# A rebuilt prologue: scale factors of the first heads apart, head 0's maxima from staged pieces, late chunks and tail squares moved into the attention slots

## The reference

```python
x = x + attn_a(_layernorm(x), Wq, Wk, Wv, bq, bk, bv, Wo, bo)   # 16 heads of 64, causal softmax
x = x + ffn(_layernorm(x), w1, b1, w2, b2)                      # relu, width 512
x = x + attn_b(_layernorm(x), W_qk, W_v, alibi_slope)           # one head of 128, causal, with a slope
x = x + ffn(_layernorm(x), w1, b1, w2, b2)

def attn_a(x, ...):
    q = einsum('bse,hed->bhsd', x, Wq) + bq;  k = ... + bk;  v = ... + bv
    scores = where(causal, einsum('bhsd,bhtd->bhst', q, k) / sqrt(64), -inf)
    out = einsum('bhst,bhtd->bhsd', softmax(scores), v)
    return out.transpose(0, 2, 1, 3).reshape(B, S, 1024) @ Wo + bo
```

## Time and profile before

| what | value |
|---|---|
| median of 3 runs | 563.73 us (562.64 to 566.23) |
| the profiled execution's own span | 561.3 us |
| TensorE busy | 526.3 us, 94% |
| ScalarE, GpSimd, VectorE busy | 469.0, 453.8, 446.3 us |
| mean granted clock of TensorE | 0.988 of full |
| prologue, until slot 0 | 35.28 us |
| slot 0 | 13.7 us |
| a slot between 72.5 and 401 us | 11.75 us |

### The profile page before, as it was taken

The page is one execution under the profiler, slowest core; times in us unless marked ns, Lnnn a source line. Parts: engine busy times, 40 slices in busy tenths (PEclk is TensorE's granted clock), DMA queues, the critical chain, the costliest instruction groups (busy, mean ns, idle before and its releaser), DMA issues.

```text
span 561.3 us, 17932 instructions
## 1 busy us (share of the span) xinstructions
PE 526.3 (94%) x6864; PEld 371.1 (66%) x6864; DVE 446.3 (80%) x1382; ACT 469.0 (84%) x925; POOL 453.8 (81%) x447
## 2 busy tenths in 40 slices
PE   4888999999999999999999999998989998798897
PEld 3654666666666666766667666675679695656576
DVE  5878888888888888888888888887785575788943
ACT  3888998999988999989999899998973978573995
POOL 5678989888888888888888888888983977654885
PEclk9979999999999999999999999999999999998999
DMA  9442343332433324333243332435147100000002
GB/s 227 109 113 57 72 110 86 96 96 68 114 87 97 95 64 118 87 95 96 60 122 80 102 97 58 124 78 198 40 151 272 68 3 2 1 1 2 1 21 57
DMA packets 35461, 48.03 MB, mean 86 GB/s; under 512 B 10777, under 2 KB 16817, under 8 KB 35377
## 3 DMA queue, kind: packets, MB, share of 16 engines
q1 hardware_dynamic: 33264, 46.35, 30.2%
q10 hardware_dynamic: 2112, 0.54, 0.4%
HBM read 12.27 MB, written 9.44 MB: 39 GB/s over the span
## 4 chain that ended last, share of the span: by engine, by line
PE 75%; DVE 8%; issue 6%; ACT 5%; POOL 5%; DMA 1%; DVEq 0%; POOLq 0%; ACTq 0%
PE psum L562 11%; PE psum L620 10%; PE psum L621 10%; PE psum L516 7%; PE psum L518 6%; PE psum L517 6%; PE psum L600 6%; PE psum L602 6%; PE psum L601 6%; PE psum L623 2%; POOL h_lo L2146 1%; PE psum L781 1%; POOL rstd L2024 1%; ACT xn L1164 1%; DVE st_lo L1515 1%
## 5 line engine op out<-in xcount | busy, mean ns | idle before, releaser
L2079 POOL TENSOR_TENSOR p_hl<-p,p_hl 128x512 f16<-128x512 f32 x288 | 328.5, 1165 | 48.4 <-ACT p_hl L1264 44.6
L1532 DVE CUSTOM_DVE_ANT_0 max_junk<-psum,mask_s 128x1024 bf16<-128x1024 f32 (+7 forms) x256 | 190.4, 753 | 32.7 <-issue 32.6
L1263 ACT ACTIVATE p<-psum 128x512 f32<-128x512 f32 x288 | 175.9, 611 | 13.8 <-PE psum L623 12.2
L1264 ACT ACTIVATE p_hl<-psum 128x512 f16<-128x512 f32 x288 | 177.2, 615 | 0.0
L620 PE MATMUL psum<-q_hl,k_hh 128*128 128x512 f16 (+3 forms) x384 | 125.6, 327 | 0.5 <-ACT p_hl L1264 0.4
L600 PE MATMUL psum<-v_all,p_hl 128*128 128x65 f16 x1152 | 124.8, 193 | 1.1 <-POOL p_hl L2079 1.0
L601 PE MATMUL psum<-v_all,p_hl 128*128 128x64 f16 x1152 | 124.9, 192 | 0.0
L602 PE MATMUL psum<-v_all,p_hl 128*128 128x65 f16 x1152 | 124.4, 194 | 0.0
L621 PE MATMUL psum<-q_hm,k_l 128*128 128x512 f16 (+3 forms) x384 | 122.3, 327 | 0.0
L600 PEld LDWEIGHTS psum<-v_all,p_hl 128*128 128x128 f16 x1152 | 107.1, 98 | 16.1 <-POOL p_hl L2079 1.2
L601 PEld LDWEIGHTS psum<-v_all,p_hl 128*128 128x128 f16 x1152 | 106.2, 97 | 4.8
(11 more groups left out here) (206 smaller groups left out, 1109.1 us busy)
## 6 DMA issues: line engine op xcount, KB each, us to landing
k_hh<-st_hi SPq DMA_DIRECT2D x64, 128.0 KB, 2.3
o_scratch<-o_sb SPq DMA_DIRECT2D x16, 512.0 KB, 2.6
o_in<-o_scratch SPq DMA_DIRECT2D x8, 1024.0 KB, 8.6
q_hl<-st_hi SPq DMA_DIRECT2D x32, 128.0 KB, 2.4
q_hl<-st_lo SPq DMA_DIRECT2D x32, 128.0 KB, 2.4
k_l<-st_lo SPq DMA_DIRECT2D x32, 128.0 KB, 2.3
q_hm<-st_hi SPq DMA_DIRECT2D x32, 128.0 KB, 2.4
x_sb<-in_L_attn_a_x SPq DMA_DIRECT2D x4, 256.0 KB, 3.9
```

The costliest lines, as they stand in the source:

```text
L1263: nc.scalar.activation(p32[:, ring_at(u, r), :], src, ACT.Exp, scale=SCALE_A).then_inc(exp_done, 1)
L1264: nc.scalar.activation(p_hl[:, u % 2, 0, BANK * r:BANK * (r + 1)], src, ACT.Exp, scale=SCALE_A).then_inc(phi_done, 1)
L1532: nc.vector.tensor_tensor_reduce(out=max_junk[:, n % 2, 0:cols], in0=max_banks(v, j, 0, cols), in1=mask_s[:, S - cols:S], scale=1.0, scala ...
L2079: nc.gpsimd.tensor_tensor(p_hl[:, u % 2, 1, cols], p32[:, ring_at(u, r), :], p_hl[:, u % 2, 0, cols], ALU.subtract)\
```

## The change

Which work stands where, part by part:

- The factors of Wk and Wq are made twice: group 0 for the first four heads (the first 256 columns, loaded first, with half of the bias columns' first four), group 1 for the other twelve, later in the prologue. The factor E is put into the squares (`scale=ROOT_E`), so `norm_kq` is one operation, and a second matmul adds the biases' sums. V's bias is loaded behind the first part of Wq.
- GpSimd's memset of k_l moves ahead of the masks, the one of q_hm goes to VectorE, the one of v_all behind the masks.
- The first four pieces come in the order 0, 2, 1, 3 and go into a staging buffer of their own (st0). Head 0's maxima are matmuls of 64 rows from st0, two for each 512 columns (high and low half of Q), in the order of tiles 3, 2, 1, 0, 7, 6, 5, 4. The moves to k_hh and so on are issued behind the fourth piece, twelve in a row, ahead of the loads of chunks 2 and 3.
- Four V units, `rest_scale` (now ScalarE's) and the sums of squares of the late heads change places: the units go into slot 0, the rest stays in the prologue between head 0's maxima. The V units no longer pass through p32 and GpSimd.
- In slot 0 TensorE waits for the bias sum (`bo_done`) first; piece 6 comes behind the first unit of scores.
- Chunks 2 and 3: statistics at the end of slots 2 and 3, power and shift on GpSimd in slots 3 and 4, normalized tiles on ScalarE in slots 5 to 8, transposing in slots 7 and 9. Tail squares: one a slot in slots 10 to 15; their sums and `tail_norm` in slot 16, `tail_gain` in slot 17, scales in 18 to 20.
- 52 idle products are left.

```diff
+    FIRST_ORDER = (0, 2, 1, 3)
+    FIRST_TILES = (3, 2, 1, 0, 7, 6, 5, 4)
+    LATE_STATS_AT = {2: 2, 3: 3}
+    LATE_RSTD_AT = {3: 2, 4: 3}
+    LATE_NORM_AT = {5: (2, 0), 6: (2, 2), 7: (3, 0), 8: (3, 2)}
+    LATE_TURN_AT = {7: 2, 9: 3}
+    SQUARE_AT = {10: 0, 11: 1, 12: 2, 13: 3, 14: 4, 15: 5}
+    SUMS_AT = 16
...
             load_x(0)
+            load_heads(0, Wk, 0, GH, wk_in[0])
             load_x(1)
...
+            load_heads(2, Wv, 0, H, wv_in)
+            load_heads(0, Wk, GH, H, wk_in[1])
...
+            sp.wait_ge(piece_hi, 4)
+            sp.wait_ge(piece_lo, 4)
+            move_k(0)
+            move_q(0)
+            move_k(1)
+            move_q(1)
             load_x(2)
             load_x(3)
...
+                    if v == 0:
+
+                        keys = st0_hi[0:DH, 0, c0:c1]
+                        nc.tensor.matmul(max_banks(v, j, c0, c1), st0_hi[0:DH, 1, P * j:P * (j + 1)], keys, start=True, stop=False)
+                        last = nc.tensor.matmul(max_banks(v, j, c0, c1), st0_lo[0:DH, 1, P * j:P * (j + 1)], keys, start=False, stop=True)
+                        continue
...
+                if v - 1 in LATE_TURN_AT:
+                    pe.wait_ge(xt_lo_done, LATE_TURN_AT[v - 1] + 1)
+                if v - 1 == SUMS_AT:
+                    pe.wait_ge(row_made, 1)
...
+                def first_unit(m):
+                    if u == 0:
+                        if m == 0:
+                            pe.wait_ge(wv_first_lo, 1)
+                        if m >= 2:
+                            pe.wait_ge(v_lo_done, m - 1)
+                        values(m, V_BANKS[m])
+
+                def late_part():
+                    if u in LATE_TURN_AT:
+                        pe.wait_ge(v_lo_done, units_after(u))
+                        turn_chunk(LATE_TURN_AT[u])
...
+            idle_products(14, 5)
...
+            norm_sums(0, MAXB + 1, 0)
+            idle_products(4, 5)
             turn_chunk(0)
+            idle_products(4, 5)
+            turn_chunk(1)
+            idle_products(6, 5)
+            for n in FIRST_ORDER:
+                pe.wait_ge(first_lo, n // 2 + 1)
+                pe.wait_ge(xt_lo_done, n % 2 + 1)
+                piece(n, FIRST_BANKS[n])
             idle_products(8, 5)
+            pe.wait_ge(piece_lo, 2)
+            max_tile(0, 0)
+            max_tile(0, 1)
+            idle_products(4, SUM_BANK, P)
...
             turn_maxima(0)
+            idle_products(12, 2)
+            for par in range(2):
+                pe.wait_ge(k_moved[par], moved_by(par))
+                pe.wait_ge(q_moved[par], moved_by(par))
+            pe.wait_ge(bo_done, 1)
...
                 outputs(1)
-                tail_weights(2)
+                if u in LATE_STATS_AT:
+                    first_stats(LATE_STATS_AT[u])
+                if u == SUMS_AT + 1:
+                    tail_gain()
...
+            nc.vector.memset(q_hm[DH:P, :, :].bitcast(F32), 0.0).then_inc(qm_zeroed, 1)
...
+            piece_low(0, FIRST_BANKS[0])
+            piece_low(2, FIRST_BANKS[2])
+            take_max(0, 0)
+            piece_low(1, FIRST_BANKS[1])
+            take_max(0, 1)
+            piece_low(3, FIRST_BANKS[3])
+            take_max(0, 2)
+            take_max(0, 3)
             norm_v()
+            take_max(0, 4)
             gain_v()
+            norm_kq(1, SUM_BANK, 2)
+            take_max(0, 5)
+            gain_kq(1)
+            first_low_v()
+            scale_bias(1)
+            piece_low(4, FIRST_BANKS[4])
+            take_max(0, 6)
+            dve.wait_ge(kq_ready, 4)
+            piece_low(5, FIRST_BANKS[5])
+            take_max(0, 7)
```

More of the change, by code:

```diff
@@ L382, in units_after, with moved_by, max_order, piece_place @@
             return min(u + FIRST_UNITS, VUNITS)
-        def moved_by(v, of_pair=48, ahead=32):
-            return of_pair * (v // 2 + 1) - (ahead if v % 2 == 0 else 0)
+        def moved_by(v, of_pair=48):
+            return of_pair * (v // 2 + 1)
+        def max_order(v):
+            return FIRST_TILES if v == 0 else MAX_ORDER
+        def piece_place(n):
+            return FIRST_ORDER.index(n) if n < len(FIRST_ORDER) else n
+        def stage(pair):
+            return (st0_hi, st0_lo) if pair == 0 else (st_hi, st_lo)
         def unit_heads(m):
@@ new lines, in _ @@
+            nc.tensor.matmul(bank(SUM_BANK)[:, 4:5], ones[:, :], sums[:, 8:9], start=True, stop=True).then_inc(frov_full, 1)
+            pe.wait_ge(piece_lo, 4)
+            max_tile(0, 4)
+            piece(4, FIRST_BANKS[4])
+            pe.wait_ge(normv_done, 1)
+            norm_sums(1, SUM_BANK, 2)
+            max_tile(0, 5)
+            piece(5, FIRST_BANKS[5])
+            pe.wait_ge(wo_in, 16)
+            pe.wait_ge(norm_done, 2)
+            for n in (6, 7):
+                max_tile(0, n)
+                for k in range(OB // 2 * (n - 6), OB // 2 * (n - 5)):
+                    last = nc.tensor.matmul(bank(SUM_BANK)[:, 8:9], wo_raw[:, k, :], b_cols[:, 2, k:k + 1], start=(k == 0), stop=(k == OB - 1))
```

460 lines of the change are left out of this document (227 added, 233 removed).

## The result

The changed kernel takes **569.31 us** (median of 4, 568.11 to 572.49), beside 563.18 for the kernel before on the same chip (561.22 to 566.23): a ratio of 1.012, 95% interval 1.0065 to 1.0173. That is 2.3 us over the 567.0 of the prediction: inside its range of 560.0 to 570.0, but above the band of its forecast, 565.3 to 568.7. It is slower by 1.2%, a little over the 1% that the prediction set as the bound; the interval has both sides of that bound.

The account below looks back on a forecast made before the run. TensorE was taken as the bound, full in slots 1 to 30, with gains only in the first 49 us. Profiled 561.3 - 2.5 + 5.8 = 564.6, and 2.4 for the median over the profile gave 567.0 us; range 560.0 to 570.0.

Parts of the forecast that it names:

- Factors at 10.0: Prologue: weight factors made from the first four heads alone would stand at 10.0 instead of 14.72, 4.7 us earlier.
- Memsets at nothing: Prologue: moving GpSimd's k_l memset ahead of the masks and q_hm's to VectorE would cost no time.
- The upper end of the prediction: Prologue: two memsets of 1.80 us that shut each other out would move the factors by 1 us.
- Pieces and first maximum: Prologue: pieces start at 11.6, 1.0 us lost to half clock, head 0's first maximum at 16.3 against 26.24.
- Maxima, the step that failed most: Prologue behind the first maximum: VectorE's work and waits summed to 31.2 instead of 35.28, 4.1 us earlier.
- Slot 0 itself: Head 0's slot: four value units come in, some work leaves, and TensorE waits for the bias sum; grows by 1.6 us.
- The slots: Slots 1 to 18: work moved there meets a full TensorE and costs 5.8 us, priced by each place's slack.
- Rival B: Slots absorb the waits and only TensorE's own 1.3 us is paid: 562.5 us; chance 0.15.
- the tail gain: Slot 17: 0.45 us ahead of the first maximum less 0.16 of slack, a cost of 0.3 us.
- Rival D: SP's twelve moves issue late, at 1.0 us on average, and hold slot 0 for 3.1 us: 570.1 us; chance 0.12.
- A: Front: TensorE's clock stays up, winning 2.3 us in slot 0 and 1.0 ahead of the pieces: 563.7 us; chance 0.17.
- C: Clock stays up and slots absorb the waits, both together: 559.2 us; chance 0.13.

Follow-up runs that it names:

- e2: Changed kernel with V's bias loaded ahead of the first part of Wq and x's second chunk ahead of Wk's first heads: 566.57 us.
- e6_all: Changed kernel plus 70 idle products, two earlier loads, tail_gain behind slot 18's first maximum, late statistics spread, bias sum ahead of head 0's q_hm: 561.34 us, ratio 0.9971.
- e1: Changed kernel with 70 more idle products between head 0's maxima, behind the output bias matmuls and ahead of slot 0: 566.76 us, ratio 1.0070.
- e11: e9 with 10 and 14 idle products behind the two groups of output bias matmuls and 18 instead of 12 ahead of slot 0: 559.84 us, ratio 0.9952.
- e8b: Changed kernel with only 16 more idle products, between head 0's narrow tiles, profiled again: 568.18 us in that execution; ratio of the kernel 1.0046.
- e7: e6_all with ScalarE's copy of the turned chunk between unit 6's two exponentials in slots 7 and 9: 561.41 us.
- e9: e6_all with only the 16 idle products between narrow tiles, and slots 7 and 9's last maximum ahead of transposes and xT_lo: 559.49 us, ratio 0.9975.

## Why the prediction was right, and where it wasn't

The time fell into the range, 0.6 us above the band of the forecast, but not with the parts as worked out. By the sums: the forecast for the profiled time was -2.5 at q_hm of head 1 and +5.8 in the slots; measured were +0.9, +7.2 and, behind the slots, +1.2.

*Factors at 10.0.* They stood at 11.86, for two loads that were mis-sized. V's bias "behind a Wq load" was taken as +0.2 us and brought the bias columns from 5.14 to 7.05; the second chunk of x, which was given 1 us of slack, came at 6.97 and VectorE with it. With both moved ahead again (e2) the factors stand at 10.60, in e6_all at 10.05. A smaller miss stood beside them: from the last square to the end of the power it was 2.17 us (8.96 to 11.13), where 1.8 was taken.

*Memsets at nothing.* Right, by these rows of the kernel after:

```profile
1.78 1.76 DVE L1755 MEMSET q_hm<- 64x2048 f32 x1 [0.48 <-issue]
...
1.93 1.80 POOL L2131 MEMSET k_l<- 64x2048 f32 x1
```

They ran side by side at full speed. The upper end of the prediction, two memsets that shut each other out, isn't so. The Trainium skill (SBUF — State Buffer, Who interferes with whom) has VectorE operations with at most one input in SBUF stay off the shared pair outside the two-port modes; the trace agrees. xn fell from 2.48 to 1.09, as taken.

*Pieces and first maximum.* From the factors to the first maximum 6.3 us were forecast and 6.02 measured, with 1.9 us of the pieces at half: right, and the first maximum was late (17.88, not 16.3) by what the factors were late.

*Maxima, the step that failed most.* From the first maximum to q_hm of head 0 the sum gives 31.2 - 1.22 - 16.3 = 13.7; it took 15.6. The prediction let the clock fall, but in slot 0, as in the earlier trace rows. It fell 11 us earlier than there, under the maxima, and stayed for 17 us. The argument it had in hand, "52 idle products are left of 104", was put to the question whether the clock falls and not when. The sum was one of VectorE's work, and in the run that wasn't the path: the chain that ended last (start, us, what) stays on TensorE from 20.88 until 34.61, nearly all of it at half clock and with 3.6 us of bias matmuls, L818, that the sum doesn't have:

```profile
20.88 0.37 PE psum L602
...
28.33 1.79 PE psum L818 x8
...
31.30 1.79 PE psum L818 x8
```

At the full clock (e1) the same stretch takes 13.1 and its chain runs mostly over VectorE and ScalarE, so the sum of 13.7 was about right for that path. Slot 0 itself was forecast at 16.6 and took 16.53.

*The slots.* Taken 1.13, 1.13, 1.35, 1.25, 0.6 and 0.3; measured 1.08, 1.07, 1.37, 1.26, 0.65 and 1.66. Five of six are within 0.06, since each was worked out at its place: the statistics from the 0.16 us of slack between VectorE's first maximum and TensorE's second, for which TensorE now waited 0.94, the turns from the chain over ScalarE and VectorE, the tail sums from TensorE's own matmuls. Rival B (absorbed waits) is out. The xn tiles, tail squares and GpSimd's rstd cost nothing, as said: slots 5, 6, 8 and 10 to 15 stay at 11.75. The term that was mis-sized is the tail gain. It was priced by the 0.17 of the kernel before, where the two operations happened to stand in a pause of GpSimd; the new place is beside eight subtractions without one.

*Behind the slots.* The change doesn't touch it, and nothing was forecast. The 1.24 us are one more stretch of 3.41 us at half clock. The experiments, whose instructions there are the same, have 0 to 10.2 us of it, so it is taken as spread and not as the change's.

*Rival D, SP's moves.* They were issued from 20.48 to 28.5, one at 1.03 and the rest at 0.6, and never held slot 0. *A and C* needed a clock that stays up; e1 is A made true, 5.4 us earlier at q_hm of head 1, 1.25 of it before the first maximum, where the prediction had counted 3.3. The clock was worth more than that, because the fall took in the maxima and not slot 0 alone.

So the time came out nearer than the parts, and that is partly luck. The profiled 570.7 is 6.1 over the 564.6 of the sum: 3.4 at q_hm of head 1 (1.9 from the loads, 1.9 from the clock, less small gains), 1.4 in the slots, nearly all of it tail_gain, and 1.2 behind them. But this execution, 572.49 us, is 3.2 over the median of its four, and it lies 1.8 over its span where 2.4 had been added: 6.1 - 3.2 - 0.6 = 2.3. Neither of these two is to the sum's credit.

The direction was right for its own reason. What leaves the prologue costs 7.1 us in slots that TensorE fills; in front the rebuilding wins 49.06 - 44.61 = 4.5 us with the clock up (e1) and 6.0 with the loads and the bias sum mended as well (e6). By this sum it needs tail_gain and the statistics in better places to win: without their 3.2 us e6_all's 561.34 would be 564.5, over the 562.21 before. With them it wins, 0.5% in e11. But the old kernel wins 0.24% (interval 0.9954 to 0.9998) by 42 idle products alone, and that interval overlaps e11's: what the rebuilding brings beyond a better kept clock isn't shown by the times.

What stays open: what either of the two loads costs by itself; why the clock fell for 17 us in the change and for 3 to 7 in e8b, e7, e9 and e11; and turning the chunks through another bank wasn't tried.

## What to carry to other kernels

When work is moved out of a prologue into a loop whose bottleneck engine is full, price each piece by the slack of its place, not by its engine's idle share: the same statistics cost 1.08 us a slot as one block in front of the first maximum and nothing in smaller blocks ahead of the fifth. When idle matmuls are removed or narrow matmuls are put first, ask when the clock will now fall and what lies under it. A tiny VectorE operation that only scales SBUF data lasted here until GpSimd's subtraction beside it ended, so look for GpSimd's pauses in the trace before giving it a place.
